# The first turn of an expert sum one group later, and a cast behind two silus, in a pipelined RWKV and mixture-of-experts kernel

## The chip, the cores and the metric

The kernel runs on one core of one Trainium2 chip. The metric is the device time of one execution in microseconds (us), less is better. TensorE multiplies and transposes, VectorE and ScalarE work elementwise, GpSimd does small sums and powers, SyncE issues the transfers.

## What is computed

Sixteen sequences of 512 tokens and 256 channels go through a layer of two halves, each with a layer norm ahead and a residual sum behind. The first half is an RWKV mix of tokens (three projections of mixtures of a token with the one before it, a scan over the tokens, an output projection). The second is a causal convolution with a pointwise product, then eight experts of which each token takes two, an output product, an RMS norm, and a feed-forward with gelu.

```python
x = x + attn(layernorm(x))
x = x + ffn(layernorm(x))
# ffn, cut:
x1 = x + silu(conv(x) @ pw)
logits = x1 @ router                       # top 2 of 8, softmax over the two
ye = silu(einsum('bsd,eod->bseo', x1, expert_w) + expert_b)
combined = einsum('bse,bseo->bso', rw, ye)
h = rmsnorm(x1 + combined @ out)
y = h + gelu(h @ down) @ up                # plus biases
```

## The kernel before

Every engine has an instruction stream of its own, written out by hand; semaphores tie the streams together, and an engine works through its stream in the written order. The order within a stream is therefore the schedule: an instruction that waits holds all that stands behind it on its engine.

The sequences are pipelined in five stages. `body(g, f, b, a, n)` emits one pass, in which five neighbouring sequences are in work: n is normalised and turned, a goes through the RWKV scan, b through its projection and second norm, f through the experts, g through the RMS norm and the feed-forward. Twenty passes are emitted; those with g from 1 to 10 are a hardware loop (`Fori`, L296), the others are straight-line code. A pass starts on TensorE with the k product of a (L624), and on VectorE with the running maximum of a (`running_maximum`, a scan, L1216) over k, which ScalarE copies out of PSUM (`copy_k`, L821) behind the squares (L805) and a table load (L906).

The expert work of sequence f has four token tiles of 128 tokens, and four groups of two experts for each tile, so sixteen groups; group i of tile t on TensorE is `experts(t, (i,))`, seven matmuls of 512 columns (L466 to L470: a bias and six products of halves in fp16) into one of two banks `pe`. ScalarE's `silus` (L776) empties a bank into one of eight buffers `ye`; a group may start when the silu of the group two before it is through. VectorE multiplies each half of a buffer by the token's weight and adds it to `comb[:, t]` (L1400, L1405). When all eight experts of a tile are in, `turn_combined(f, t)` on TensorE transposes the sum (L490), and `copy_combined` on ScalarE copies it out (L793) for the output product `mix_out` (L511). Ahead of the groups stand the router's products (L684 to L688), which need the high and the low half of x1 (`x1h` by ScalarE, L970, `x1l` by VectorE, L1311).

In the same pass ScalarE runs gelu for sequence g (L978), casts its result to fp16 (`ffs`, L980) and once more the upper 64 rows of it (`ffh`, L981); each raises `ffh_ready` by one. VectorE waits for the first of them (L1363), and TensorE's up product (`feed_up`, behind groups 0 and 1 of tile 1) for both. ScalarE then loads the table set of silu (L983), runs the silus of the first two groups, copies x2 to `x2t` (L989), which VectorE's residual sum of the next sequence waits for (L1144), and computes the tanh for the routing weights (L994).

Of the kernel before, what the change touches and what calls it, by code (L numbers as in the profile page):

```python
# [47 lines left out]
def build(nc, x, vecs, w_attn, w_pw, w_router, w_expert, w_out, w_down, w_up, b_rows, b_down, norm_w, out):  # L48
# [4 lines left out]
    HID = w_down.shape[1]  # L53
# [6 lines left out]
    with ExitStack() as ctx:  # L60
        def sb(name, shape, dt=F32):
            return ctx.enter_context(nc.sbuf_tensor(name, shape, dt))
# [4 lines left out]
        def sig(name, per):  # L67
            return Signal(ctx.enter_context(nc.semaphore(name)), per)
# [102 lines left out]
        ffg = sb("ffg", [2 * HID, T])  # L171
        ffs = sb("ffs", [2 * HID, T], F16)
        ffh = sb("ffh", [HID + 2, T], F16)
# [80 lines left out]
        ffh_ready = sig("ffh_ready", 2)  # L254
# [13 lines left out]
        def sums(t, n):  # L268

            return t * (NE - 1) + n + 1  # L270

        def on(seq):

            return not isinstance(seq, int) or 0 <= seq < B
# [166 lines left out]
        def _(te):  # L441
# [13 lines left out]
            def body(g, f, b, a, n):  # L455
                draining = on(f) and not on(a)

                def experts(t, groups=range(NG)):
                    tok = slice(t * P, (t + 1) * P)
                    for grp in groups:  # L460
                        i = t * NG + grp

                        if ye_ready.rises(f, i - 1):
                            te.wait_ge(ye_ready.sem, ye_ready.at(f, i - 1))
                        dst, cols = pe[:, i % 2, :], slice(grp * T, (grp + 1) * T)
                        nc.tensor.matmul(dst, ones2[:], brow[:, cols], start=True, stop=False)  # L466
                        for h in range(H):
                            nc.tensor.matmul(dst, x1h[:, h, tok], weh[:, h, cols], start=False, stop=False)  # L468
                            nc.tensor.matmul(dst, x1h[:, h, tok], wel[:, h, cols], start=False, stop=False)  # L469
                            mm = nc.tensor.matmul(dst, x1l[:, h, tok], weh[:, h, cols], start=False, stop=h == H - 1)  # L470
                        mm.then_inc(expert_done.sem, 1)

                def turn_combined(seq, t):

                    te.wait_ge(combined.sem, combined.at(seq, sums(t, NE - 1)))


                    if t < 2:
                        if on(n):
                            te.wait_ge(xt1_ready.sem, xt1_ready.at(n, t + 1))  # L480
                        if on(g):
                            te.wait_ge(ffg_ready.sem, ffg_ready.at(g))
                        if t == 1 and on(b):
                            te.wait_ge(xt2_ready.sem, xt2_ready.at(b, 2))
                    else:
                        te.wait_ge(combt_ready.sem, combt_ready.at(seq, t - 1))
                        if on(seq + 1):
                            te.wait_ge(xt2_ready.sem, xt2_ready.at(seq + 1, t - 1))
                    for h in range(H):
                        mm = nc.tensor.transpose(pt[:, t % 2, h * P:(h + 1) * P], comb[:, t, h * P:(h + 1) * P],  # L490
                                                 ident[:])
                    mm.then_inc(t3_done.sem, 1)
# [204 lines left out]
                    turn_front()  # L697
                if on(f):
                    experts(1, (3,))
                    turn_combined(f, 0)  # L700
                    experts(2)
                    experts(3, (0, 1))
                if on(b):
                    turn_proj()
# [23 lines left out]
        def _(act):  # L728
# [4 lines left out]
            def body(g, f, b, a, n):  # L733
                draining = on(f) and not on(a)

                def fade(m, h):

                    act.wait_ge(xt1_ready.sem, xt1_ready.at(n, h + 1))
                    if on(a):
                        act.wait_ge(kvr_done.sem, kvr_done.at(a, H * (m + 1)))  # L740
                    act.activation((xk, xv, xr)[m][:, h, :], xt1[:, h, 0:T], ACT.Identity,
                                   scale=keep[:, m, h:h + 1]).then_inc(faded[m].sem, 1)
# [17 lines left out]
                def normalise_front(tiles):  # L760
                    normalise(n, xa, rstd1, shift1, xn1, rstd1_ready, xn1_ready, t1_done, tiles)

                def normalise_proj(tiles):
                    normalise(b, x2, rstd2, shift2, xn2, rstd2_ready, xn2_ready, t2_done, tiles)

                def silus(t, groups):
                    for grp in groups:
                        i = t * NG + grp
                        act.wait_ge(expert_done.sem, expert_done.at(f, i + 1))

                        if i >= NY:
                            old_t, old_grp = (i - NY) // NG, (i - NY) % NG
                            act.wait_ge(combined.sem, combined.at(f, sums(old_t, EPG * old_grp + EPG - 1)))
                        elif on(g):
                            act.wait_ge(combined.sem, combined.at(g))
                        act.activation(ye[:, i % NY, :], pe[:, i % 2, :], ACT.Silu,  # L776
                                       scale=1.0 / WSCALE).then_inc(ye_ready.sem, 1)

                def begin_combined(t):

                    act.wait_ge(route.sem, route.at(f))
                    act.wait_ge(ye_ready.sem, ye_ready.at(f, t * NG + 1))
                    if on(g):
                        act.wait_ge(t3_done.sem, t3_done.at(g, t + 1))
                    act.activation(comb[:, t, :], ye[:, t * NG % NY, 0:C], ACT.Identity,  # L785
                                   scale=rw[:, t, 0:1]).then_inc(comb_begun.sem, 1)

                def copy_combined(seq, t):
                    act.wait_ge(t3_done.sem, t3_done.at(seq, t + 1))

                    if on(seq - 1):
                        act.wait_ge(moe_done.sem, moe_done.at(seq - 1))
                    act.copy(combt[:, :, t * P:(t + 1) * P],  # L793
                             pt[:, t % 2, 0:C].rearrange("p (h k) -> p h k", h=H)).then_inc(combt_ready.sem, 1)
# [176 lines left out]
                if on(g):  # L971
                    act.preload_act_table_set("gelu_and_others")  # L972
                    act.wait_ge(down_done.sem, down_done.at(g))

                    if on(g - 1):
                        act.wait_ge(ffl_ready.sem, ffl_ready.at(g - 1))
                        act.wait_ge(up_done.sem, up_done.at(g - 1))
                    act.activation(ffg[:], pt[:, 0, :], ACT.Gelu, bias=bdown[:, 0:1]).then_inc(ffg_ready.sem, 1)  # L978
                    act.wait_ge(ffg_ready.sem, ffg_ready.at(g))
                    act.copy(ffs[:], ffg[:]).then_inc(ffh_ready.sem, 1)  # L980
                    act.copy(ffh[0:HID, :], ffg[0:HID, :]).then_inc(ffh_ready.sem, 1)  # L981
                if on(f):
                    act.preload_act_table_set("silu_and_others")  # L983
                    silus(0, (0, 1))

                    act.wait_ge(x2_ready.sem, x2_ready.at(f))
                    if on(g):
                        act.wait_ge(xh_ready.sem, xh_ready.at(g))
                    act.copy(x2t[:], x2[:]).then_inc(x2t_ready.sem, 1)  # L989

                    act.wait_ge(route.sem, route.at(f, 1))
                    if on(g):
                        act.wait_ge(route.sem, route.at(g))
                    act.activation(th[:], gap[:], ACT.Tanh, scale=0.5 / WSCALE).then_inc(tanh_ready.sem, 1)  # L994
                    for i in range(2, 6):
                        silus(i // NG, (i % NG,))
                        if on(n):
                            normalise_front((i - 2,))
                    begin_combined(1)
                    silus(1, (2,))  # L1000
                if on(n):
                    copy_front()
                if on(f):
                    silus(1, (3,))
                    if on(n):
                        fade(0, 0)
                    copy_combined(f, 0)
                    silus(2, (0,))
                    if on(n):
                        fade(0, 1)  # L1010
                    for i in range(1, NG + 1):
                        silus(2 + i // NG, (i % NG,))
                        if i == 1:
                            begin_combined(2)
                        if on(b):
                            normalise_proj((i - 1,))
                    begin_combined(3)
                    silus(3, (1,))
# [443 lines left out]
```

## Time and profile before

| | before |
|---|---|
| median of 3 runs | 955.78 us (953.82 to 956.95) |
| the profiled execution | 956.12 us, its span 954.30 us |
| TensorE busy | 879.2 us (92%) in 4292 matmuls |
| VectorE busy | 847.5 us (89%) in 1533 instructions |
| ScalarE busy | 741.1 us (78%) in 1285 instructions |
| GpSimd busy | 214.0 us (22%) in 472 instructions |

The page is read like this: a busy time is the sum of the recorded durations, a share is that of the span. Matmuls are pipelined and their ends are modelled, so whether TensorE waits is read from the starts of its matmuls. A line number is that of the listing above. In a timeline the figure in brackets is how long the engine was idle just before, with what ended it.

### The profile page before, as it was taken

What the parts mean: (1) busy time and instruction counts of PE and PEld (TensorE: products, weight loads), DVE (VectorE), ACT (ScalarE), POOL (GpSimd) and SP (SyncE); (2) the same over time, 40 slices, a digit from 0 to 9 for tenths busy, and PEclk for the clock granted to TensorE, in tenths of its full rate; (3) what the DMA queues carried; (4) which work ended last, traced back from release to release, by engine and by line L of the source; (5) the groups of instructions that cost most, each with busy time, mean ns of one, the idle gap of its engine ahead of it and who ended that gap; (6) DMA issues with size and microseconds to landing.
All of it is one profiled execution on the core that took longest, in us unless ns stands there. A gap on an engine that the chain in (4) does not pass through costs nothing. (4 is left out here: it accounts for less than half of the span.)

```text
span 954.3 us, 15851 instructions
## 1 busy us (share of the span) xinstructions
PE 879.2 (92%) x4292; PEld 480.8 (50%) x4292; DVE 847.5 (89%) x1533; ACT 741.1 (78%) x1285; POOL 214.0 (22%) x472
## 2 busy tenths in 40 slices
PE   1676999999999999999999999999999999979896
PEld 0232555555555555554555555455555555445543
DVE  4998899999999999999999999999999999967663
ACT  3748798887879888787888878787988878665653
POOL 5260312212131122213131221313022221201100
PEclk9887999999999999999999999999999999999998
DMA  6110100102010010101010010201001010100000
GB/s 216 45 44 1 45 1 1 67 1 67 0 44 22 14 52 0 66 0 66 0 44 22 0 66 0 66 0 44 22 0 65 1 45 1 45 0 24 0 24 22
DMA packets 28789, 29.67 MB, mean 31 GB/s; under 512 B 2106, under 2 KB 28500, under 8 KB 28500
## 3 DMA queue, kind: packets, MB, share of 16 engines
q1 hardware_dynamic: 28756, 29.27, 9.2%
q8 instruction: 15, 0.25, 0.1%
q14 instruction: 18, 0.15, 0.0%
HBM read 20.87 MB, written 8.39 MB: 31 GB/s over the span
## 5 line engine op out<-in xcount | busy, mean ns | idle before, releaser
L776 ACT ACTIVATE ye<-pe 128x512 f32<-128x512 f32 x256 | 151.3, 597 | 112.1 <-PE pe L470 108.6
L1405 DVE SCALAR_TENSOR_TENSOR comb<-ye,rw,comb 128x256 f32<-128x256 f32 x448 | 214.9, 482 | 20.6 <-ACT comb L785 5.8
L470 PE MATMUL pe<-weh,x1l 128*128 128x512 f16 x512 | 194.0, 379 | 0.0
L469 PE MATMUL pe<-wel,x1h 128*128 128x512 f16 x512 | 194.0, 379 | 0.0
L468 PE MATMUL pe<-weh,x1h 128*128 128x512 f16 x512 | 194.0, 379 | 0.0
L466 PE MATMUL pe<-brow,ones 128*128 128x512 f16 x256 | 97.1, 379 | 4.0 <-ACT ye L776 4.0
L421 POOL TENSOR_TENSOR msv<-ms,rms_eps_c 128x2 f32<-128x2 f32 x32 | 10.9, 341 | 373.9 <-ACT sq L805 373.9
L392 POOL TENSOR_TENSOR mo<-st 128x4 f32<-128x4 f32 x32 | 10.0, 312 | 340.5 <-DVE st L1189 197.2
L470 PEld LDWEIGHTS pe<-weh,x1l 128*128 128x128 f16 x512 | 50.1, 98 | 60.4
L469 PEld LDWEIGHTS pe<-wel,x1h 128*128 128x128 f16 x512 | 50.0, 98 | 60.5
L468 PEld LDWEIGHTS pe<-weh,x1h 128*128 128x128 f16 x512 | 50.1, 98 | 50.5
L451 PE MATMUL pk<-xk,wa 128*128 128x512 f32 x128 | 64.5, 651 | 9.9 <-issue 7.0
L511 PE MATMUL po<-wout,combt 128*128 128x256 f32 x256 | 70.2, 397 | 0.0
L445 PE MATMUL pt<-ident,xn 128*128 128x128 f32 x256 | 36.5, 289 | 33.7 <-ACT xn L757 22.7
L451 PE MATMUL pk<-cv,wpw 128*128 128x512 f32 x128 | 61.4, 603 | 2.0 <-DVE cv L1161 2.0
L451 PE MATMUL pk<-xr,wa 128*128 128x512 f32 x128 | 58.2, 597 | 2.4 <-DVE xr L1169 2.4
L451 PE MATMUL pk<-xv,wa 128*128 128x512 f32 x128 | 58.8, 602 | 0.9 <-ACT kk L821 0.9
L537 PE MATMUL po<-wo,rwkv 128*128 128x256 f32 x256 | 57.9, 379 | 0.0
L537 PEld LDWEIGHTS po<-wo,rwkv 128*128 128x128 f32 x256 | 48.6, 190 | 13.4 <-issue 7.7
L445 PEld LDWEIGHTS pt<-ident,xn 128*128 128x128 f32 x256 | 31.0, 149 | 42.9 <-issue 33.2
L1207 DVE SCALAR_TENSOR_TENSOR hh<-po,rms,normw 128x256 f32<-128x256 f32 x64 | 28.0, 478 | 24.1 <-POOL rms L425 24.0
L405 POOL TENSOR_TENSOR pw<-mo,minus_half 128x4 f32<-128x4 f32 x32 | 47.0, 1470 | 2.5
(169 smaller groups left out, 1953.5 us busy)
## 6 DMA issues: line engine op xcount, KB each, us to landing
xa<-in_x SPq DMA_DIRECT2D x16, 512.0 KB, 3.5
xres<-in_x SPq DMA_DIRECT2D x16, 512.0 KB, 4.3
out_y<-yo SPq DMA_DIRECT2D x15, 512.0 KB, 2.9
ye<-in_w_expert SPq DMA_DIRECT2D x2, 1024.0 KB, 8.0
wa<-in_w_attn SPq DMA_DIRECT2D x1, 1024.0 KB, 11.5
out_y<-yo SPq DMA_DIRECT2D x2, 256.0 KB, 2.1
wpw<-in_w_pw SPq DMA_DIRECT2D x1, 256.0 KB, 11.6
wout<-in_w_out SPq DMA_DIRECT2D x1, 256.0 KB, 7.0
```

Of the source, the lines that this page charges most:

```text
L405: nc.gpsimd.tensor_tensor(pw[:, 0], mo[:, 3], minus_half[:], ALU.pow).then_inc(ready.sem, 1)
L445: mm = nc.tensor.transpose(pt[:, h, t * P:(t + 1) * P], src[:, t, h * P:(h + 1) * P], ident[:])
L451: mm = nc.tensor.matmul(dst, weight[:, h, m * P:(m + 1) * P], src[:, h, :], start=h == 0, stop=h == H - 1)
L466: nc.tensor.matmul(dst, ones2[:], brow[:, cols], start=True, stop=False)
L468: nc.tensor.matmul(dst, x1h[:, h, tok], weh[:, h, cols], start=False, stop=False)
L469: nc.tensor.matmul(dst, x1h[:, h, tok], wel[:, h, cols], start=False, stop=False)
L470: mm = nc.tensor.matmul(dst, x1l[:, h, tok], weh[:, h, cols], start=False, stop=h == H - 1)
L511: mm = nc.tensor.matmul(dst, combt[:, h, tok], wout[:, h, :], start=False, stop=h == H - 1)
L537: mm = nc.tensor.matmul(po[:, i, t % 2, :], rwkv[:, h, t * P:(t + 1) * P], wo2[:, h, :], start=h == 0, stop=h == H - 1)
L776: act.activation(ye[:, i % NY, :], pe[:, i % 2, :], ACT.Silu, scale=1.0 / WSCALE).then_inc(ye_ready.sem, 1)
L1207: v.scalar_tensor_tensor(out=hh[:, t, :], in0=po[:, i, t % 2, :], scalar=rms[:, t:t + 1], in1=normw[:], op0=ALU.mult, op1=ALU.mult).then_i ...
L1405: v.scalar_tensor_tensor(out=comb[:, t, :], in0=src, scalar=rw[:, t, e:e + 1], in1=comb[:, t, :], op0=ALU.mult, op1=ALU.add).then_inc(comb ...
```

## The change

On TensorE the first group of tile 2 is issued ahead of the turn of tile 0's sum, where it stood behind it. On ScalarE the silu of that group goes ahead of the copy of the turned sum, likewise. And on ScalarE the cast of the upper half, `ffh`, which stood ahead of the load of silu's table, goes behind the silus of the first two groups. The work itself is the same.

```diff
@@ -697,8 +697,9 @@
                 if on(f):
                     experts(1, (3,))
+                    experts(2, (0,))
                     turn_combined(f, 0)
-                    experts(2)
+                    experts(2, (1, 2, 3))
                     experts(3, (0, 1))
@@ -978,10 +979,12 @@
                     act.activation(ffg[:], pt[:, 0, :], ACT.Gelu, bias=bdown[:, 0:1]).then_inc(ffg_ready.sem, 1)
                     act.wait_ge(ffg_ready.sem, ffg_ready.at(g))
                     act.copy(ffs[:], ffg[:]).then_inc(ffh_ready.sem, 1)
-                    act.copy(ffh[0:HID, :], ffg[0:HID, :]).then_inc(ffh_ready.sem, 1)
                 if on(f):
                     act.preload_act_table_set("silu_and_others")
                     silus(0, (0, 1))
+                if on(g):
+                    act.copy(ffh[0:HID, :], ffg[0:HID, :]).then_inc(ffh_ready.sem, 1)
+                if on(f):
 
                     act.wait_ge(x2_ready.sem, x2_ready.at(f))
@@ -1004,8 +1007,8 @@
                     silus(1, (3,))
                     if on(n):
                         fade(0, 0)
+                    silus(2, (0,))
                     copy_combined(f, 0)
-                    silus(2, (0,))
```

## Rows read from the trace of the kernel before

**Rows 1.** One loop pass: us, busy us (instructions) by engine, clock, DMA

```profile
430.06:484.76 54.70, 54.04 (x275) 29.62 (x271) 52.15 (x95) 46.06 (x81) 12.20 (x28) 1.00 0.08 29
```

**Rows 2.** Waits: engine, line, waited for: us in total, times, longest

```profile
DVE pp L1216 <- ACT kk L821: 7.6, 13, 1.1
...
PE pt L490 <- DVE comb L1405: 5.7, 13, 0.8
...
PE pe L466 <- ACT ye L776: 4.0, 14, 0.4
```

**Rows 3.** Timeline, TensorE: start us, us, engine, line, operation, count [idle before]

```profile
432.65 0.38 PE L469 MATMUL pe<-wel,x1h 128*128 128x512 f16 x1
432.86 0.38 PE L470 MATMUL pe<-weh,x1l 128*128 128x512 f16 x1
433.50 0.39 PE L466 MATMUL pe<-brow,ones 128*128 128x512 f16 x1 [0.25 <-ACT ye L776]
```

**Rows 4.** Timeline, ScalarE, from x1's casts to the third expert silu

```profile
427.14 1.22 ACT L970 CAST x1h<-x 128x512 f16<-128x512 f32 x2 [0.18 <-DVE x L1305]
428.38 1.28 ACT L972 ACT_TABLE_LOAD   x1
...
430.39 0.62 ACT L980 CAST ffs<-ffg 128x512 f16<-128x512 f32 x1
430.92 0.61 ACT L981 CAST ffh<-ffg 64x512 f16<-64x512 f32 x1
431.55 1.28 ACT L983 ACT_TABLE_LOAD   x1
432.84 1.08 ACT L776 ACTIVATE ye<-pe 128x512 f32<-128x512 f32 x2
433.81 1.05 ACT L989 COPY x2t<-x 128x1024 f32<-128x1024 f32 x1
...
435.22 0.60 ACT L776 ACTIVATE ye<-pe 128x512 f32<-128x512 f32 x1 [0.25 <-PE pe L470]
```

**Rows 5.** Timeline, VectorE and TensorE, at the turn of the first sum

```profile
443.66 1.01 DVE L1405 SCALAR_TENSOR_TENSOR comb<-ye,rw,comb 128x256 f32<-128x256 f32 x2
...
444.91 0.41 PE L490 MATMUL pt<-ident,comb 128*128 128x128 f32 x2 [0.41 <-DVE comb L1405]
```

**Rows 6.** Timeline, VectorE and ScalarE, at the start of a loop pass

```profile
408.43 1.00 DVE L1405 SCALAR_TENSOR_TENSOR comb<-ye,rw,comb 128x256 f32<-128x256 f32 x2
...
409.32 0.59 ACT L821 COPY kk<-pk 128x512 f32<-128x512 f32 x1
...
409.94 1.23 DVE L1216 TENSOR_TENSOR_SCAN pp<-decay,kk 128x512 f32<-128x512 f32 x1 [0.51 <-ACT kk L821]
```

**Rows 7.** Line L1215, 409 to 410: sequencer, ns min/median/max, first and last start

```profile
L1215 DVEq FUSED_REGOPS  x1: 64/64/64, 409.4 to 409.4; - x1
```

**Rows 8.** Timeline, VectorE and TensorE, at the router products

```profile
427.96 1.29 DVE L1311 TENSOR_TENSOR x1l<-x,x1h 128x512 f16<-128x512 f32 x2 [0.25 <-ACT x1h L970]
...
429.36 0.17 PE L684 MATMUL pk<-brow,ones 128*128 128x8 f16 x1
```

**Rows 9.** Timeline, VectorE, the residual sum of the next sequence

```profile
436.26 0.67 DVE L1144 TENSOR_TENSOR x<-po,xres 128x512 f32<-128x512 f32 x1
```

**Rows 10.** Timeline, VectorE, the same place in pass 1, ahead of the loop

```profile
190.26 1.00 DVE L1405 SCALAR_TENSOR_TENSOR comb<-ye,rw,comb 128x256 f32<-128x256 f32 x2
191.17 1.22 DVE L1216 TENSOR_TENSOR_SCAN pp<-decay,kk 128x512 f32<-128x512 f32 x1
```

**Rows 11.** Timelines, TensorE and VectorE, in passes 0, 13 and 15

```profile
117.19 0.44 PE L490 MATMUL pt<-ident,comb 128*128 128x128 f32 x2 [0.56 <-DVE comb L1405]
...
136.81 2.34 DVE L1216 TENSOR_TENSOR_SCAN pp<-decay,kk 128x512 f32<-128x512 f32 x2 [1.14 <-ACT kk L821]
...
856.34 0.88 DVE L1207 SCALAR_TENSOR_TENSOR hh<-po,rms,normw 128x256 f32<-128x256 f32 x2 [8.50 <-POOL rms L425]
...
911.26 0.39 PE L466 MATMUL pe<-brow,ones 128*128 128x512 f16 x1 [0.36 <-ACT ye L776]
```

## The prediction

> **What bounds the kernel now.** I read the page first, then one pass of the loop by itself, then who waits for whom, and last the timelines of the engines around the waits. The page shows TensorE and VectorE both near full, so a shorter wait on one of them can be swallowed by the other. The row of one loop pass says the same: in 54.70 us TensorE is busy 54.04 us at a granted clock of 1.00 (the level of 2.4 GHz, so no clock effect is in the sum) and VectorE 52.15 us in 95 instructions [rows 1]. There are ten such passes; with the straight-line ones before and behind the loop, sixteen passes work on experts. I number them 0 to 15; the loop holds 2 to 11.
>
> TensorE's busy time hides its waits, since a 512-column matmul is recorded as 0.38 us while the next one starts 0.215 us later. The waits show in the starts: 0.215 us between two matmuls of a group, but 0.64 us (433.50 - 432.86) ahead of the third expert group of a sequence, which waits for ScalarE's first silu. So 0.42 us are lost there; the 0.25 us in brackets plus the overlap of 0.165 us gives the same [rows 3]. The list of waits has this one 14 times [rows 2]. The second wait stands ahead of the turn of the first expert sum: 0.41 us in brackets plus 0.165 us are 0.575 us, ended by VectorE's combination, which ran 443.66 to 444.67 [rows 5]; 13 times in the list [rows 2]. Together TensorE loses 0.99 us a loop pass at the two places that the diff touches.
>
> VectorE waits too: its scan for the running maximum (L1216), the first instruction of a loop pass, starts 0.51 us after the combinations end, held by ScalarE's copy of k [rows 6], 13 times [rows 2]. That copy follows TensorE's k product, the squares and a table load. So the ring is: x1's low half is ready on VectorE (427.96 + 1.29 = 429.25), TensorE's router products start at 429.36, right behind it [rows 8], then the expert groups with the two waits, the k product, ScalarE's copy of k, VectorE's scan, and VectorE without a pause until the next low half. A microsecond taken from the first half of this ring counts until VectorE has no wait left at the scan.
>
> **Part 1: the upper half cast behind the first two silus.** The casts of one pass start at 430.39 and 430.92 and the table load for silu at 431.55, where the second cast ends; the pair of silus starts at 432.84 [rows 4]. Without the second cast the load starts where the first one ends, 430.39 + 0.62 = 431.01, so 0.54 us earlier, and the first silu runs 432.31 to 432.9. TensorE wants the bank at 432.86 + 0.215 = 433.08. The handover took 0.06 us (silu one 432.84 + 0.60, matmul 433.50), so the bank is free at 432.97 and the 0.42 us vanish with 0.1 us to spare.
>
> The cast does not vanish. The second silu can't start ahead of its own matmuls (the last one ends at 432.86 + 0.38 = 433.24, so about 433.3, where it also was before). Then come the cast (a slot of 430.92 - 430.39 = 0.53 us) and the x2 copy, which starts at 433.3 + 0.49 + 0.53 = 434.3 instead of 433.81 [rows 4]. Queued behind these on ScalarE are the tanh for the routing weights and the third silu. The distance from the x2 copy to the third silu was 435.22 - 433.81 = 1.41 us, of which 0.25 us was a wait for matmuls, so the third silu starts at 434.3 + 1.16 = 435.5 and ends at 436.1. TensorE, now unstalled, wants that bank for the fifth group at 433.08 + 14 x 0.2155 = 436.10. New wait: 0 to 0.1 us; I take 0.04. The x2 copy ends at 435.4; VectorE's residual add, which needs it, stands at 436.26 [rows 9], so a cover of 1.4 us shrinks to 0.9 us. The up product needs both casts only several groups later; it loses nothing. No DMA is issued or moved, and nothing moves in the queues of GpSimd or SP.
>
> **Part 2: the turn behind the ninth expert group.** The same two transposes and the same copy, issued one group of 7 x 0.2155 = 1.51 us later on TensorE, and on ScalarE the ninth silu ahead of the copy. With part 1 alone TensorE would come to the turn 0.4 us earlier and wait 0.4 us longer, as VectorE's sum is where it was. With the group between them TensorE arrives 0.99 us early minus 1.51 us, so 0.5 us after the sum is there, and the 0.575 us go. The ninth group needs the bank of the seventh, whose silu is long done. ScalarE's copy of the turned sum is used much later by the output product; the ninth silu ahead of it starts when its own group ends. I cost the swap at nothing.
>
> **What becomes of 0.95 us.** TensorE (0.99 - 0.04) brings the k copy up to 0.95 us earlier. VectorE can use only what it waits at the scan. The bracket says 0.51 us, but a loop edge lies there: VectorE's sequencer runs the branch, and its last register instruction for the scan's wait starts at 409.4 and takes 0.064 us [rows 7], while the scan starts at 409.94 [rows 6]. With k early, the scan starts right behind that, at about 409.55: a gain of 0.38 us a pass. Upper bound: in pass 1, outside the loop's edge, the scan follows the pair of combinations after 191.17 - 190.26 = 0.91 us [rows 10]; in the loop it is 409.94 - 408.43 = 1.51 us, so at most 0.60 us. Lower bound: the register row is given to 0.1 us, so 0.33 us. I take 0.38, as its row is of this very edge. From there VectorE is the bound, and TensorE's other 0.5 us turn into a longer wait ahead of the router products. VectorE's small waits further on stay: they hang on VectorE's own results.
>
> Here a rule of the Trainium skill leads elsewhere. Perfetto Trace Analysis, section Optimization Strategies, says that where the matmul engine sits idle for others, the engines blocking it are to be sped up so that it keeps going. By that rule the whole 0.95 us a pass would be gained (rival A); the row of VectorE's 0.51 us speaks against it, as less is to be had there than TensorE has to give.
>
> **Sum.** Passes 2 to 12 have the scan's wait, 11 x 0.38 = 4.2 us (I price pass 11 and 12, at and behind the loop's end, as one of the loop). Pass 1 has none, since VectorE goes straight on [rows 10]: 0. Pass 0 has no gelu, but its turn waits 0.56 + 0.165 = 0.72 us, and its scan 1.14 us, so all of the 0.72 us counts [rows 11]. Pass 13 is bound by VectorE's combinations and then by the chain through GpSimd, shown by VectorE's 8.50 us wait [rows 11]: 0. Pass 14 has neither wait: 0. In pass 15 TensorE bounds the tail, and its third group waits 0.36 + 0.165 = 0.52 us [rows 11]; all of it lies on the chain that ended last: 0.5 us. Together 4.2 + 0.7 + 0.5 = 5.4 us. The profiled execution took 956.12 us (span 954.30 and 1.82 around it), so it would be 950.7, its span 948.9. It stood 0.34 us above the median of the runs, 955.78, so I predict a median of **950.4 us**. With the bounds of 0.33 and 0.60 us a pass the same sum gives 951.0 to 948.0.
>
> **Rivals.** A: VectorE gives way as well (some of its waits behind the scan close too), and TensorE's full gain counts: 11 x 0.95 + 1.2 = 11.7 us, 944.1 us. For it: TensorE is the fuller engine. Against it: 52.15 us of VectorE work in 95 instructions with a small pause between each leave no 0.9 us a pass.
> B: the scan waits for the loop edge and not for k; then nothing is gained in the loop but what the edge allows, say 0.1 us a pass: 955.8 - 1.1 - 1.2 = 953.5, within 0.3% of before (2.87 us). A measurement of this kernel can tell about that much from no change. For it: the register row is only 0.5 us ahead of the scan. Against it: the scan's wait names the copy of k, which runs 409.32 to 409.91, and the scan starts 0.03 us behind that [rows 6].
> C, the slower side: the cast doesn't run under silu's table, so the table would be swapped there and back, two loads of 1.28 us [rows 4]. The x2 copy and the third silu then come 2.6 us later; the fifth group stalls 2.6 us where 0.99 us was saved, so each of about 14 passes loses 1.6 us: 978 us. It decides from 0.95 us of delay on. Against it: the casts of x1 are of the same form and run between the silu of the pointwise product and the next table load, with none of their own [rows 4].
>
> **Chances.** My forecast, anywhere in 947.5 to 952.3: 0.78. A: 0.05. B: 0.12. C: 0.02. Another small slip that costs what is gained, slower by little: 0.03. The range that leaves out 2 in 10 takes in the bounds (948.0, 951.0) and reaches some way to A and to B: 946.8 to 953.2. Faster by over 0.3% is the forecast and A and a little of B: 0.85; within 0.3%: 0.12; slower: 0.03.
>
> **What would show it.** In the profile after: no wait ahead of the third expert group and of the first turn; the silu load right behind the first cast; no wait for k at the scan; a loop pass near 54.3 us; TensorE's idle time ahead of the router products grown to about 0.6 us. If the pass is near 53.8, A holds; if it stays at 54.6, B. The prediction is wrong if the scan still waits for k, because then ScalarE and not TensorE sets when k is copied, or if VectorE's instructions themselves change in length when the engines stand differently to each other.

## The result and the profile after

| | before | after |
|---|---|---|
| median of 8 runs each, same chip | 956.7 us (953.82 to 961.45) | 948.25 us (942.25 to 952.72) |
| the profiled execution, its span | 956.12 us, 954.30 us | 952.72 us, 950.9 us |
| one loop pass (start of the first expert group to the next) | 54.70 us | 54.27 us |
| VectorE busy in a loop pass | 52.15 us | 52.10 us |

The ratio is 0.9905 with an interval of [0.9879, 0.9931]: faster by 6.6 to 11.6 us. A second comparison of the same two kernels, on another occasion, gave 947.15 us (8 runs) against 954.6 us, 0.9929 [0.9904, 0.9954], or 4.4 to 9.2 us. The two intervals overlap from 6.6 to 9.2 us. The forecast was a median of 950.4 us, in a range of 946.8 to 953.2.

The loop pass of the kernel after, which answers [rows 1] (stretch, its length, then busy time and instructions of TensorE, its weight loads, VectorE, ScalarE and GpSimd, the granted clock, the DMA share, GB/s):

```profile
430.22:484.48 54.26, 53.97 (x274) 29.66 (x271) 52.10 (x95) 45.96 (x81) 13.33 (x28) 1.00 0.09 29
```

The same work takes 0.43 us less a pass, at the same full clock. The next three fences are timelines (start, us, engine, line, operation; a wait ahead of it in brackets). TensorE at the third expert group and at the turn of the first sum, which answers [rows 3, 5]:

```profile
433.02 0.38 PE L470 MATMUL pe<-weh,x1l 128*128 128x512 f16 x1
433.24 0.38 PE L466 MATMUL pe<-brow,ones 128*128 128x512 f16 x1
...
445.36 0.38 PE L470 MATMUL pe<-weh,x1l 128*128 128x512 f16 x1
445.58 0.38 PE L490 MATMUL pt<-ident,comb 128*128 128x128 f32 x2
```

Both times the next matmul starts 0.22 us behind the one ahead, as within a group. Before it was 0.64 us at the third group, and the turn had 0.41 us in brackets. Both waits are gone. ScalarE, which answers [rows 4]:

```profile
430.55 0.62 ACT L981 CAST ffs<-ffg 128x512 f16<-128x512 f32 x1
431.19 1.28 ACT L983 ACT_TABLE_LOAD   x1
432.48 0.60 ACT L777 ACTIVATE ye<-pe 128x512 f32<-128x512 f32 x1
433.44 0.60 ACT L777 ACTIVATE ye<-pe 128x512 f32<-128x512 f32 x1 [0.36 <-PE pe L470]
433.93 0.60 ACT L986 CAST ffh<-ffg 64x512 f16<-64x512 f32 x1
434.44 1.04 ACT L992 COPY x2t<-x 128x1024 f32<-128x1024 f32 x1
435.49 0.57 ACT L777 ACTIVATE ye<-pe 128x512 f32<-128x512 f32 x1
```

The load of silu's table stands right behind the first cast, the moved cast runs at 433.93 under silu's table, and the third silu starts as soon as the x2 copy ends. VectorE at the start of the next pass, which answers [rows 6]:

```profile
463.28 1.00 DVE L1408 SCALAR_TENSOR_TENSOR comb<-ye,rw,comb 128x256 f32<-128x256 f32 x2
464.41 1.23 DVE L1219 TENSOR_TENSOR_SCAN pp<-decay,kk 128x512 f32<-128x512 f32 x1
```

Before, the scan started 1.51 us behind the start of the last two combinations and named the copy of k; now it is 1.13 us and there is no bracket. The register instruction ahead of the scan, which answers [rows 7] (shortest, median and longest duration in ns, first and last start), is what it now follows:

```profile
L1218 DVEq FUSED_REGOPS  x1: 64/64/64, 464.3 to 464.3; - x1
```

TensorE does not run through, however. It has two waits that the kernel before did not have, one ahead of the k product and one ahead of the xr product; the first row of each pair is the matmul ahead, and VectorE's mix that makes the operand stands below:

```profile
459.88 0.38 PE L470 MATMUL pe<-weh,x1l 128*128 128x512 f16 x1
460.42 1.55 PE L451 MATMUL pk<-xk,wa 128*128 128x512 f32 x3 [0.16 <-issue]
...
470.11 0.38 PE L511 MATMUL po<-wout,combt 128*128 128x256 f32 x1
470.62 0.70 PE L451 MATMUL pk<-xr,wa 128*128 128x512 f32 x1
...
458.67 1.41 DVE L1172 SCALAR_TENSOR_TENSOR xk<-xt,vec,xk 128x512 f32<-128x512 f32 x2
...
469.16 1.41 DVE L1172 SCALAR_TENSOR_TENSOR xr<-xt,vec,xr 128x512 f32<-128x512 f32 x2
```

In the kernel before, the k product follows the expert matmuls without a pause, 1.03 us behind the end of the mix (458.52 + 1.41 = 459.93):

```profile
458.52 1.41 DVE L1169 SCALAR_TENSOR_TENSOR xk<-xt,vec,xk 128x512 f32<-128x512 f32 x2
...
460.96 1.45 PE L451 MATMUL pk<-xk,wa 128*128 128x512 f32 x3
```

Now it starts 0.54 us behind the last expert matmul instead of 0.22, so it waits 0.32 us. The trace puts this down to "issue", but VectorE's mix of xk ends at 458.67 + 1.41 = 460.08, and TensorE's register instruction of line 620, which waits for that mix, starts at 460.1. Those of lines 622 and 623, for two more waits of the k product, follow:

```profile
L620 PEldq FUSED_REGOPS  x1: 51/51/51, 460.1 to 460.1; - x1
...
L622 PEldq FUSED_REGOPS  x1: 37/37/37, 460.2 to 460.2; - x1
...
L623 PEldq ALU_OP  x1: 36/36/36, 460.3 to 460.3; - x1
```

The Trainium skill, "Perfetto Trace Analysis", section Per-engine timelines, says that the profiler's window of an instruction which only the sequencer runs opens when its semaphores are satisfied. By that reading 460.1 is the end of a wait, and the row agrees, as it falls on the end of the mix. The mix itself was not late: the matmul was due at 459.88 + 0.22 = 460.10. The 0.32 us are the way from the end of that wait through the three instructions to the matmul, 0.34 us from the end of the mix. In the kernel before, line 620 opened at 460.0, also right behind the mix, and the same three instructions ran while TensorE still had expert matmuls to do.

The xr product starts 0.51 us behind a matmul that in the kernel before was followed after 0.2 us, so it waits 0.30 us. Here the mix is late, and the product comes 0.05 us behind its end (469.16 + 1.41 = 470.57), with no such instruction between. Of the 0.99 us a pass that TensorE lost at the two places of the change, 0.43 became time and some 0.6 went here.

### The profile page after: what moved, and what is told of

Read it like the earlier page. It is cut to its first block, busy times and chain, and to the rows that moved or that the text cites. A ratio compares the mean times of both kernels' runs of the same rounds, so it can differ in the third digit from the quotient of the medians.

```text
span 950.9 us, 15851 instructions
## 1 busy us (share of the span) xinstructions
PE 881.5 (93%) x4292; PEld 483.4 (51%) x4292; DVE 846.6 (89%) x1533; ACT 740.1 (78%) x1285; POOL 231.1 (24%) x472
## 4 chain that ended last, share of the span: by engine, by line
PE 53%; DVE 25%; issue 13%; ACT 4%; POOL 4%; DVEq 1%; DMA 0%; SPq 0%; ACTq 0%; POOLq 0%
PE pk L451 13%; DVE comb L1408 9%; PE pe L470 6%; PE pe L468 6%; PE pe L469 6%; PE po L537 5%; PE pt L445 3%; PE pe L466 3%; PE pt L665 3%; DVE xr L1172 2%; DVE pp L1219 2%; PE po L511 2%; DVE yo L1183 2%; DVE num L1128 2%; DVE gd L1228 2%
## 5 line engine op out<-in xcount | busy, mean ns | idle before, releaser
L421 POOL TENSOR_TENSOR msv<-ms,rms_eps_c 128x2 f32<-128x2 f32 x32 | 17.4, 545 | 355.0 <-ACT sq L806 355.0
L451 PE MATMUL pk<-xr,wa 128*128 128x512 f32 x128 | 60.6, 617 | 3.9 <-DVE xr L1172 2.8
L758 ACT ACTIVATE xn<-xa,shift,rstd 128x256 f32<-128x256 f32 x64 | 36.9, 590 | 14.6 <-POOL shift L410 14.6
## 6 DMA issues: line engine op xcount, KB each, us to landing
wa<-in_w_attn SPq DMA_DIRECT2D x1, 1024.0 KB, 11.6
```

The costliest lines, as they stand in the source:

```text
L451: mm = nc.tensor.matmul(dst, weight[:, h, m * P:(m + 1) * P], src[:, h, :], start=h == 0, stop=h == H - 1)
L758: act.activation(dst[:, t, :], src[:, t, :], ACT.Identity, scale=rs[:, t:t + 1], bias=shift[:, t:t + 1]).then_inc(ready.sem, 1)
```

## The experiments

The theory: the change closes both waits of TensorE, VectorE then holds the pass at the loop edge, and TensorE's other half is spare. The rivals: TensorE still sets the pass (A), or the loop edge did all along and little can be gained (B). The first two runs do one part of the change alone; three load or unload one engine of the changed kernel; one repeats it; the last three shorten VectorE's path for good, each alone and both together. The loop pass is the measure wherever only one run was taken, as it repeats to 0.02 us while whole executions differ by several us.

**The cast alone.** The kernel before, with the cast moved and the turn left where it was.

```diff
-                    act.copy(ffh[0:HID, :], ffg[0:HID, :]).then_inc(ffh_ready.sem, 1)
                 if on(f):
                     act.preload_act_table_set("silu_and_others")
                     silus(0, (0, 1))
+                if on(g):
+                    act.copy(ffh[0:HID, :], ffg[0:HID, :]).then_inc(ffh_ready.sem, 1)
+                if on(f):
```

> Only the cast is moved; the turn stands where it stood before. My theory (VectorE's first expert sum gates the turn): TensorE comes to the turn 0.42 us earlier and waits 0.99 us there instead of 0.57, so a loop pass stays at 54.70 us; only the last expert pass gains 0.5 us. Time within 0.1% of before. Rival (a wait of TensorE counts wherever it is taken away): a loop pass of 54.3 us, about 4 us less in all.

Measured: 955.47 us against 954.76, ratio 0.9995 [0.9967, 1.0024], a loop pass of 54.70 us. TensorE at the turn:

```profile
443.27 0.38 PE L470 MATMUL pe<-weh,x1l 128*128 128x512 f16 x1
444.49 0.41 PE L490 MATMUL pt<-ident,comb 128*128 128x128 f32 x2 [0.84 <-DVE comb L1407]
```

From 443.27 the turn was due at 443.49 and starts at 444.49: a wait of 1.00 us where it was 0.575. The 0.42 us saved at the third group are lost 11 us later, to the same sum by VectorE. So the cast alone is worth nothing in the loop; the half microsecond that was to be seen in the last pass is not seen above the spread.

**The turn alone.** The kernel before with the turn, its copy and the ninth silu swapped, and the cast left.

```diff
                     experts(1, (3,))
+                    experts(2, (0,))
                     turn_combined(f, 0)
-                    experts(2)
+                    experts(2, (1, 2, 3))
...
-                    copy_combined(f, 0)
                     silus(2, (0,))
+                    copy_combined(f, 0)
```

> Only the turn (with its silu and copy) is moved; the cast stands ahead of the table load as before, so the third expert group still waits 0.42 us. Theory (VectorE is the bound from 54.27 us a pass on, and TensorE needs to give only about 0.4 of its 0.99 us): a loop pass of 54.27 to 54.4 us, so this part alone brings nearly all of the loop's gain, and the parts do not add up. Rival (the gains add, each part with its share): 54.45 to 54.5 us.

Measured: 949.29 us against 954.76, 0.9944 [0.9913, 0.9974]. The loop pass, and TensorE at the third group:

```profile
423.50:477.78 54.28, 54.02 (x275) 29.63 (x272) 52.12 (x95) 46.13 (x81) 12.66 (x28) 1.00 0.08 29
```

```profile
426.30 0.38 PE L470 MATMUL pe<-weh,x1l 128*128 128x512 f16 x1
426.94 0.39 PE L466 MATMUL pe<-brow,ones 128*128 128x512 f16 x1 [0.26 <-ACT ye L777]
```

The wait of 0.42 us at the third group stays (0.64 us between the starts), and still the pass is as short as with the whole change. The turn alone frees 0.575 us, more than the 0.43 that VectorE lets through. Inside the loop the parts do not add: 0, 0.42 and 0.43 us.

**More for VectorE.** The changed kernel with one unrelated operation of 256 columns behind VectorE's last combination of a pass.

```diff
+                    if on(n):
+                        if on(n - 5) or not isinstance(n, int):
+                            dve.wait_ge(spared.sem, spared.at(g - 1))
+                        v.scalar_tensor_tensor(out=spare[:], in0=normw[:], scalar=one[:, 0:1], in1=normw[:],
+                                               op0=ALU.mult, op1=ALU.add).then_inc(spared.sem, 1)
```

> The changed kernel with one more VectorE instruction a pass, 256 columns into a tile that nobody reads, behind the last combination; the output is unchanged. Theory (VectorE bounds the loop pass): its whole slot of about 0.40 us is added, 54.67 us a pass. Rival A (TensorE bounds it and VectorE has slack): 54.27 us, unchanged.

Measured: 951.95 us (one run), a loop pass of 54.46 us, longer by 0.20 where 0.40 was expected and 0 by rival A. The rows show why it is half:

```profile
461.37 1.00 DVE L1410 SCALAR_TENSOR_TENSOR comb<-ye,rw,comb 128x256 f32<-128x256 f32 x2
462.28 0.48 DVE L1430 SCALAR_TENSOR_TENSOR spare<-normw,one 128x256 f32<-128x256 f32 x1
462.68 1.22 DVE L1221 TENSOR_TENSOR_SCAN pp<-decay,kk 128x512 f32<-128x512 f32 x1
```

The scan follows the extra operation after 462.68 - 462.28 = 0.40 us, the spacing of two VectorE operations of this size without a wait between them. The second combination of a pair starts 0.51 us behind the first (the operation behind the pair comes after 462.28 - 461.37 = 0.91 us, less 0.40). In the changed kernel that is 463.28 + 0.51 = 463.79, and the scan starts at 464.41, 0.62 us later. So the loop edge costs VectorE 0.22 us there, and those 0.22 us now run under the extra operation, which waits for nothing. That VectorE bounds the pass is confirmed; the size was missed by this.

**More for TensorE.** The changed kernel with the bias matmul of a sequence's eleventh expert group issued twice (0.215 us a pass; the second one overwrites the first).

```diff
+                        if i == 10:
+                            nc.tensor.matmul(dst, ones2[:], brow[:, cols], start=True, stop=True)
                         nc.tensor.matmul(dst, ones2[:], brow[:, cols], start=True, stop=False)
```

> The changed kernel with one more TensorE matmul of 512 columns a pass (the bias of group 10 is written twice), 0.215 us; the output is unchanged. Theory (VectorE bounds the loop pass and TensorE waits 0.32 us at the k product and 0.30 us at the xr product): hidden, 54.27 us a pass, with the wait at the k product down to about 0.1 us. Rival A (TensorE bounds it): 54.48 us.

Measured: 947.3 us (one run). The loop pass, and the k product:

```profile
426.25:480.55 54.30, 54.16 (x276) 29.74 (x273) 52.14 (x95) 46.11 (x81) 13.15 (x28) 1.00 0.08 29
```

```profile
456.12 0.38 PE L472 MATMUL pe<-weh,x1l 128*128 128x512 f16 x1
456.46 0.69 PE L451 MATMUL pk<-xk,wa 128*128 128x512 f32 x1
```

The pass stays at 54.30, and the wait ahead of the k product falls from 0.32 to 456.46 - 456.12 - 0.215 = 0.13 us. The extra matmul goes into the wait: the product again starts 0.34 us behind the end of the mix of xk (456.12). TensorE has time to spare there; rival A asked for 0.2 us more a pass.

**Less for VectorE.** The changed kernel with a mix of xv that leaves out half of its columns.

```diff
+                        w = T // 2 if m == 1 else T
-                        v.scalar_tensor_tensor(out=dst[:, h, :], in0=xt1[:, h, 1:1 + T], scalar=vec[:, 2 + m, h:h + 1],
-                                               in1=dst[:, h, :], op0=ALU.mult, op1=ALU.add).then_inc(mixed.sem, 1)
+                        v.scalar_tensor_tensor(out=dst[:, h, 0:w], in0=xt1[:, h, 1:1 + w], scalar=vec[:, 2 + m, h:h + 1],
+                                               in1=dst[:, h, 0:w], op0=ALU.mult, op1=ALU.add).then_inc(mixed.sem, 1)
```

> The changed kernel with half of VectorE's work left out in the two instructions that mix x for the v product (256 of 512 columns each), so the v product reads columns that are not fully mixed; about 0.53 us less VectorE work a pass, all of it ahead of the scan. Theory (VectorE bounds the loop pass at 54.27 us, TensorE keeps 0.30 us of wait at the xr product): the pass falls by those 0.30 us to about 53.97 us, and then TensorE bounds it. Rival A (TensorE bounds it already): 54.27 us. A scan still held by the copy of k would show as a wait for ScalarE there and a fall of less than 0.1 us.

Measured: 945.43 us (one run), and

```profile
426.22:480.19 53.97, 53.79 (x275) 29.76 (x271) 51.63 (x95) 45.98 (x81) 12.29 (x28) 1.00 0.09 29
```

The pass falls to 53.97, as expected for a pass that VectorE holds, and the wait ahead of the xr product is gone. Of the 0.53 us of work left out, 0.30 us come back, and then the product of xr no longer waits. With the two runs above this is a test from both sides: less VectorE work shortens the pass, more VectorE work lengthens it, more TensorE work does nothing.

**The changed kernel once more**, on the chip of the next run.

> The changed kernel once more, unaltered, for its median beside the others of this set and for a second trace. Theory: loop passes of 54.27 us again, and 5 to 8 us less than before, of which 0.43 us a pass lie in the loop; the rest differs from trace to trace with the stretches at the lower clock at the two ends of the program. Rival (the whole 8 us are the change's): the same head and tail as in the first trace of it.

Measured: 947.15 us (944.25 to 951.24, 8 runs), a loop pass of 54.28 us. The head, up to the first expert group, is 98.7 us in this trace against 106.2 in the first one, so the rival is out: a part of the difference between two executions is not the change's.

**The first term of tile 0 on ScalarE.** If VectorE is the bound, work taken from it is time. In the changed kernel ScalarE makes the first term of three of the four sums; here it makes tile 0's as well, behind the sixth silu, and the statistics of the projection stand ahead of VectorE's combinations.

```diff
                         silus(i // NG, (i % NG,))
+                        if i == 5:
+                            begin_combined(0)
...
+                    if on(b):
+                        stats_proj()
                     for t in range(NT):
...
-                                if e == 0 and t > 0:
-                                    dve.wait_ge(comb_begun.sem, comb_begun.at(f, t))
-                                elif e == 0:
-                                    ...
-                                    v.tensor_scalar(comb[:, t, :], src, rw[:, t, 0:1], None,
-                                                    ALU.mult).then_inc(combined.sem, 1)
+                                if e == 0:
+                                    dve.wait_ge(comb_begun.sem, comb_begun.at(f, t + 1))
...
```

> A version meant to beat both: the changed kernel, with the first term of tile 0's sum made by ScalarE, as it is for tiles 1 to 3, and the statistics of x2 ahead of the combinations, so that they cover the time of that term. VectorE loses one instruction (a slot of 0.39 us) and a wait of 0.22 us a pass, early in the pass, ahead of xk's mix for which the k product waits. Theory (VectorE bounds the pass): 54.27 - 0.6 = 53.67 us a pass, TensorE's waits at the k and the xr product near zero; about 6 us less than the changed kernel in all. Rival A: 54.27 us, unchanged.

Measured: 941.49 us (939.82 to 948.58, 6 runs) against 954.6, 0.9876 [0.9841, 0.9910]. The loop pass:

```profile
422.89:476.72 53.83, 53.83 (x274) 29.67 (x271) 51.86 (x94) 46.36 (x82) 12.66 (x28) 1.00 0.09 29
```

It fell by 0.44 us, where 0.6 was expected. Two combinations of one tile depend on each other and start 0.52 us apart, where an unrelated operation of this size lets the next start after 0.40; with the statistics taken out from between them, more of them stand in one chain. A wait of 0.14 us ahead of the xr product stays.

**The loop edge covered.** The changed kernel with the steps of the scan's second half stood behind other expert groups, so that the last of them (the product of num) comes between the last combination and the loop edge.

```diff
-        WKV_AT = {3: 5, 5: 6, 7: 7, 8: 8, 10: 9}
+        WKV_AT = {5: 5, 8: 6, 9: 7, 10: 8, 15: 9}
```

> The changed kernel with VectorE's five long steps of the scan's quotient moved within the pass, behind groups 5, 8, 9, 10 and 15 instead of 3, 5, 7, 8 and 10, so that the last instruction ahead of the loop's branch waits for nothing and the sequencer can run the branch under it. In the changed kernel the scan starts 0.62 us after the start of the last combination, with the extra instruction of the second experiment 0.40 us after it: 0.22 us are the branch. A third long step inside a tile's chain of combinations saves another 0.12 us (0.52 us from one combination to the next, 0.40 us to another instruction). Theory (VectorE bounds, and the branch stands on its path): 54.27 - 0.34 = 53.93 us a pass. Rival (the branch only showed because VectorE waited anyway, or TensorE bounds): 54.15 to 54.27 us.

Measured: 946.17 us (one run), a loop pass of 53.92 as expected. The loop pass, and VectorE around the edge:

```profile
427.17:481.08 53.91, 53.85 (x274) 29.75 (x271) 51.92 (x95) 45.96 (x81) 12.42 (x28) 1.00 0.09 29
```

```profile
458.97 1.00 DVE L1408 SCALAR_TENSOR_TENSOR comb<-ye,rw,comb 128x256 f32<-128x256 f32 x2
459.88 1.22 DVE L1136 SCALAR_TENSOR_TENSOR num<-tr,num 128x1024 f32<-128x1024 f32 x1
461.02 1.22 DVE L1219 TENSOR_TENSOR_SCAN pp<-decay,kk 128x512 f32<-128x512 f32 x1
```

The operation behind the combinations starts 0.91 us after the pair, not 1.13, and the scan follows it after 1.14 us, without a pause. That is the edge's 0.22 us. The rest is the step that was expected to be hidden in a tile's chain of combinations: in the trace 18 combinations of a pass of the changed kernel start about 0.52 us behind the one they depend on, here 17, and the one less is worth 0.52 - 0.40 = 0.12 us.

**Both.** The two last edits together.

> The version with the first term on ScalarE (53.83 us a pass, TensorE still waiting 0.14 us at the xr product) and the long steps moved as in the run beside it. Theory: VectorE would allow 53.83 - 0.34 = 53.5 us, but TensorE has only the 0.14 us left at the xr product, so TensorE takes over as the bound at about 53.65 to 53.7 us a pass; 1.5 to 2 us less than with the first term alone. Rival (VectorE still bounds): 53.5 us.

Measured: 941.41 us (938.74 to 942.83, 5 runs) against 956.35, **0.9843 [0.9818, 0.9868]**, the shortest loop pass of all here; the median alone does not tell it from that of the first term on ScalarE (941.49 us, on another chip). The loop pass:

```profile
425.09:478.77 53.68, 53.68 (x274) 29.76 (x271) 51.78 (x94) 46.38 (x82) 11.14 (x28) 1.00 0.09 29
```

TensorE is busy for the whole pass, and the wait ahead of the xr product is gone. Each edit alone gave 0.44 and 0.35 us, both give 0.59: the bound has come back to TensorE. This is the pattern of the change itself once more, one engine further round the ring.

## Why the prediction was right, point by point

**The two waits.** Right at both places. The third silu was put at 435.5 and came at 435.49; the fifth group does not wait at all, where 0.04 us were taken. Rival C fell with the cast at 433.93, which runs without a table load of its own.

**The loop pass.** The mechanism was right, and the term of 0.38 us a pass measured 0.43 us, within its bounds of 0.33 and 0.60. Counted from the start of x1's low half, the scan comes 36.68 us later in the kernel before (409.94 + 54.70 - 427.96) and 36.29 us in the kernel after (464.41 - 428.12), so 0.39 us earlier, which is the term:

```profile
428.12 1.29 DVE L1314 TENSOR_TENSOR x1l<-x,x1h 128x512 f16<-128x512 f32 x2 [0.25 <-ACT x1h L971]
...
429.15 0.38 PE L537 MATMUL po<-wo,rwkv 128*128 128x256 f32 x1
429.51 0.17 PE L684 MATMUL pk<-brow,ones 128*128 128x8 f16 x1
```

The other 0.04 us lie between another scan of VectorE (`aa`, L1106) and the sum that makes x1, 425.18 to 426.42 in the one kernel and 425.38 to 426.58 in the other. That VectorE took only what the edge left it, and that rival A's full gain stayed out, is shown by the three runs that load and unload the engines. The rule of the Trainium skill ("Perfetto Trace Analysis", section Optimization Strategies) was weighed in the prediction by its result of 0.95 us a pass; the measurement decides for 0.43. Rival B had a true core: the edge does hold the scan, but from 0.39 us earlier on, and was not what held it before.

**The step that failed** is the place of TensorE's other half microsecond. The prediction put it in "a longer wait ahead of the router products", about 0.6 us. That wait stayed at 0.15 us (429.51 - 429.15 less 0.215, in the rows above), and the time went to the k product (0.32) and the xr product (0.30), ahead of them in the pass. The ring had been drawn with one handover from VectorE to TensorE, at x1's low half. There are two earlier ones, the mixes of xk and xr, which had cover before and lost it when TensorE came earlier: the first stall falls to the first handover that has lost its cover, not to the one at which the ring was cut. At the xr product the mix is late; at the k product it is in time, and the instructions behind its wait are not. The sum did not depend on it, since VectorE sets the pass either way. With its wait the k product comes 30.20 us into the pass (460.42 - 430.22) instead of 30.90 (460.96 - 430.06), so 0.70 us earlier and not 0.95, which is still more than VectorE can use.

**The other passes.** Lengths read from the trace, in us:

| | before | after | difference | predicted |
|---|---|---|---|---|
| pass 0 | 53.30 | 52.52 | -0.78 | -0.7 |
| pass 1 | 54.43 | 54.41 | -0.02 | 0 |
| passes 2 to 10 | 492.3 | 488.4 | -3.87 | -3.4 |
| pass 11 | 54.65 | 53.85 | -0.80 | -0.38 |
| pass 12 | 54.54 | 54.17 | -0.37 | -0.38 |
| passes 13 and 14 | 94.97 | 94.48 | -0.49 | 0 |
| pass 15 to the end | 46.58 | 46.85 | +0.27 | -0.5 |

Pass 11, the last of the loop, was priced as one of the loop and gave twice that. VectorE at its end, in the kernel after:

```profile
734.62 1.00 DVE L1408 SCALAR_TENSOR_TENSOR comb<-ye,rw,comb 128x256 f32<-128x256 f32 x2
735.54 2.33 DVE L1219 TENSOR_TENSOR_SCAN pp<-decay,kk 128x512 f32<-128x512 f32 x2
```

It runs on into the code behind the loop, so the scan follows the pair after 0.92 us, as in [rows 10], and not after the loop's 1.13: no edge holds it. It was 1.58 us there before, held by the copy of k as in [rows 6]:

```profile
736.62 1.00 DVE L1405 SCALAR_TENSOR_TENSOR comb<-ye,rw,comb 128x256 f32<-128x256 f32 x2
738.20 1.23 DVE L1216 TENSOR_TENSOR_SCAN pp<-decay,kk 128x512 f32<-128x512 f32 x1 [0.58 <-ACT kk L821]
```

The term for this pass should have been taken from [rows 10], whose upper bound of 0.60 us is near the 0.66 that it gave. Passes 13 and 14 vary: 94.97 and 95.22 us in the kernel before and in that with the cast alone, 94.48 and 94.17 in two executions of the changed kernel, 94.25 in that with the turn alone. So they are shorter wherever the turn was moved, where the prediction put nothing; what shortens them was not settled. In the last pass the wait of the third group did go, but the stretch to the end was 46.85 us in one execution and 45.92 in the other, so its half microsecond can neither be shown nor denied.

**The total.** Passes 0 to 12 fell by 5.8 us against 4.9 predicted, and that is the gain for which the trace has a cause. The two intervals ask for 6.6 to 9.2, so 0.8 us or more has no cause that was shown; passes 13 and 14 may hold half a microsecond of it. Between the two profiled executions it was only 3.4 us, because the head, up to the first expert group, was 2.6 us longer in that of the kernel after, although no instruction of it had changed. So the forecast of the loop was near for the right reason. That the total came near owes something to luck as well, as pass 11 and passes 13 and 14 gave 0.9 us more than was priced and the 0.5 us of the last pass is not seen. One profile of each kernel would have been a poor witness of the sum.

## What to carry to other kernels

An idle gap on the fuller engine is worth no more than the slack that the next engine in the ring has at the handover that follows: look up that slack first (here some 0.4 of 0.99 us), and do not add the gains of two gaps that share it, as the turn alone brought what both brought. When a gap closes, go through all operands that the same engine gets from the new bound, in order of time, since the wait comes back at the first of them that has lost its cover, and count the instructions that stand behind each wait (from the operand to the matmul 0.34 us at the k product, 0.05 us at the xr product). And where a loop edge has become the bound, put an operation that waits for nothing right ahead of it; here that, with a small operation given to an engine with room, was worth another 0.59 us a pass.

## What the runs showed of the hardware that was not expected

**The edge of a loop.** Behind an operation that itself waits for a result, the loop edge cost VectorE 0.22 us (0.62 us from the last combination to the scan, 0.40 behind an operation without a wait). The scan behind the loop, where there is no edge, follows the pair 0.21 us sooner than the one in it (0.92 against 1.13 us). With an operation without a wait ahead of the edge it cost nothing, in two kernels. One reading is that the sequencer runs ahead only as far as it has no wait to hold. The instructions of the loop edge (line 296) fit it: in the kernel after they start at 463.8 to 464.2, behind the start of the last combination at 463.79, and in the kernel with the edge covered at 459.7 to 460.0, around the start of the product of num at 459.88. No run here tested it by itself.

**The way from a wait to the matmul is longer inside the loop.** In nine of the ten loop passes of the kernel after, the k product starts 0.34 us behind the end of the mix of xk, with the three register instructions between; in the first it comes later, at 0.50 us. In the two passes behind the loop, which are straight-line code, no register instruction lies between, and it starts 0.05 us behind the mix (730.01 + 1.41 = 731.42 in the first of them):

```profile
730.01 1.41 DVE L1172 SCALAR_TENSOR_TENSOR xk<-xt,vec,xk 128x512 f32<-128x512 f32 x2
...
731.48 0.70 PE L451 MATMUL pk<-xk,wa 128*128 128x512 f32 x1
```

One reading is that the counts waited for change from pass to pass in the loop, and so have to be worked out in registers; no run here took these instructions out of the loop.

**The head of the kernel is not the same each time.** The first expert group started at 98.7 to 106.2 us in the traces of these kernels, though the code of the head is the same in the kernel after and its repetition. Most of it is decided in the first 16 us. GpSimd and VectorE in the first execution of the kernel after:

```profile
10.09 2.27 POOL L407 TENSOR_TENSOR rstd<-pw,sqrt_c 128x4 f32<-128x4 f32 x1
...
8.75 1.23 DVE L1094 TENSOR_SCALAR weh<-ye 128x2048 f16<-128x2048 f32 x1 [2.10 <-DMA ye<-in_w_expert]
10.01 2.29 DVE L1096 SCALAR_TENSOR_TENSOR wel<-ye,weh 128x2048 f16<-128x2048 f32 x1
```

and in its repetition:

```profile
8.73 0.20 POOL L407 TENSOR_TENSOR rstd<-pw,sqrt_c 128x4 f32<-128x4 f32 x1
...
9.16 0.20 POOL L410 TENSOR_TENSOR shift<-mo,pw 128x4 f32<-128x4 f32 x1
...
9.56 1.23 DVE L1094 TENSOR_SCALAR weh<-ye 128x2048 f16<-128x2048 f32 x1 [3.40 <-DMA ye<-in_w_expert]
```

GpSimd's operation on four columns (lines 407 and 410) takes 0.20 us alone, and 2.25 to 2.27 us beside VectorE's conversion of the expert weights; it then ends 0.06 us behind VectorE's (10.09 + 2.27 = 12.36 against 10.01 + 2.29 = 12.30; the next such pair, at 13.57 and 13.47, ends at 15.82 and 15.76). In the repetition the weights landed 0.8 us later, GpSimd was done with the first sequence's norm by then, and TensorE's first matmul started at 11.68 us instead of 18.14: 6.5 us of the 7.5 by which the heads differ. The Trainium skill, "SBUF — State Buffer", section Who interferes with whom, states that a VectorE instruction with two inputs in SBUF contends with a GpSimd instruction that reads SBUF, and that the shared ports are an exclusive lock, so that the one that comes second is blocked until the first is done; the rows agree, with the two ends 0.06 us apart. A race between a transfer and a chain of small operations thus moves the whole kernel by several us. No run held the conversion back until that norm is done, so what it would gain in the median is open.
